# A state-space scan on one core: GpSimd multiplies the states by the C row in pairs of channel blocks

## The reference

```python
def step(state, xs):                       # 4 sequences of 512 positions
    d_t, B_t, C_t, u_t = xs                # 512 channels, 16 states each
    dA = exp(d_t[..., None] * A)
    state = state * dA + (d_t * u_t)[..., None] * B_t[:, None, :]
    y_t = einsum('ben,bn->be', state, C_t)
    return state, y_t
y = (y + D * u) * silu(layernorm(x))
x = x + tanh(g_xattn) * y
x = x + tanh(g_ffn) * moe(layernorm(x))    # top 6 of 16 experts, and two shared ones
```

## Time and profile before

| | us |
|---|---|
| median of 3 runs | 1610.62 (1610.51 to 1610.87) |
| the profiled execution's own time | 1612.12 |
| its span in the profile | 1610.3 |
| TensorE busy | 1371.0 (85%) |
| weight load busy | 1216.4 (76%) |
| GpSimd busy | 966.0 (60%) |
| VectorE busy | 812.2 (50%) |
| ScalarE busy | 781.2 (49%) |

### The profile page before, as it was taken

How to read it: one execution, slowest core, us unless ns; L and a number is a source line. 1 busy time by engine, 2 the same in 40 slices (tenths; PEclk the granted TensorE clock), 3 DMA queues, 4 the chain that set the end, 5 groups by cost and what they waited for, 6 DMA issues and landing times.

```text
span 1610.3 us, 31484 instructions
## 1 busy us (share of the span) xinstructions
PE 1371.0 (85%) x8088; PEld 1216.4 (76%) x8089; DVE 812.2 (50%) x1451; ACT 781.2 (49%) x1303; POOL 966.0 (60%) x658
## 2 busy tenths in 40 slices
PE   4477687677867776999979999999999999999993
PEld 1266576565656665988979999999999989999893
DVE  3586895887798585255223333333333333333331
ACT  2699687968768872433223333333333333323331
POOL 0276575656667685787855556666665655666631
PEclk9598798888978788999989999999999999999997
DMA  2212121112213123345363555555544555555445
GB/s 78 58 33 67 33 66 53 55 44 62 54 54 115 34 75 115 47 109 129 68 133 68 135 135 135 135 135 131 130 121 85 132 144 128 130 134 135 80 66 131
DMA packets 61040, 151.77 MB, mean 94 GB/s; under 512 B 13808, under 2 KB 14448, under 8 KB 58592
## 3 DMA queue, kind: packets, MB, share of 16 engines
q0 software_dynamic: 31024, 64.19, 21.4%
q1 hardware_dynamic: 29952, 86.78, 16.7%
HBM read 106.02 MB, written 49.25 MB: 96 GB/s over the span
## 4 chain that ended last, share of the span: by engine, by line
PE 50%; DVE 5%; POOL 5%; issue 4%; ACT 3%; DVEq 1%; ACTq 1%; DMA 0%; POOLq 0%
PE bank L1446 15%; PE bank L1426 14%; PE bank L1427 13%; PE bank L1414 3%; POOL token_lists L824 2%; PE bank L1435 2%; DVE hs L962 1%; POOL sums L811 1%; PE bank L1337 1%; ACT gt L643 1%; PE bank L1325 1%; DVEq L1159 1%; POOL w L790 1%; ACT dA L648 1%; POOL hc L758 1%
## 5 line engine op out<-in xcount | busy, mean ns | idle before, releaser
L758 POOL TENSOR_TENSOR hc<-hs,crow 128x512 f32<-128x512 f32 x256 | 322.1, 1284 | 190.3 <-DVE hs L962 148.8
L1426 PE MATMUL bank<-w,xh 128*128 (+1 forms) x1088 | 370.0, 341 | 8.6 <-DVE xl L1146 5.7
L962 DVE TENSOR_TENSOR_SCAN hs<-dA,bank 128x512 f32<-128x512 f32 x256 | 298.2, 1207 | 109.8 <-ACT dA L648 62.6
L1427 PE MATMUL bank<-w,xh 128*128 (+1 forms) x1088 | 353.1, 325 | 0.0
L811 POOL DMA_INDIRECT sums<-ys,aid x104 | 174.7, 1680 | 267.8 <-ACT ys L696 253.9
L1337 PE MATMUL bank<-ident,gt 128*128 128x128 f32 x1024 | 193.0, 320 | 131.9 <-DVE hs L962 67.5
L1446 PE MATMUL bank<-w,ah 128*128 (+1 forms) x816 | 268.9, 411 | 15.4 <-DVE al L1179 15.3
L1337 PEld LDWEIGHTS bank<-ident,gt 128*128 128x128 f32 x1024 | 140.5, 165 | 169.2 <-DVE hs L962 87.4
L1179 DVE TENSOR_TENSOR al<-bank,ah 128x384 fp32r<-128x384 f32 x136 | 75.9, 558 | 336.8 <-ACT ah L690 324.1
L1426 PEld LDWEIGHTS bank<-w,xh 128*128 128x128 f32 x1088 | 206.1, 189 | 33.2 <-issue 30.1
L1427 PEld LDWEIGHTS bank<-w,xh 128*128 128x128 f32 x1088 | 207.9, 191 | 2.4
(11 more groups left out here) (174 smaller groups left out, 1959.7 us busy)
## 6 DMA issues: line engine op xcount, KB each, us to landing
wraw<-in_wall SPq DMA_DIRECT2D x18, 2176.0 KB, 9.1
crow<-c_rows SPq DMA_DIRECT2D x64, 256.0 KB, 3.3
xt<-token_rows SPq DMA_DIRECT2D x32, 266.0 KB, 2.8
token_rows<-rowb SPq DMA_DIRECT2D x4, 1064.0 KB, 5.6
xrow<-in_x SPq DMA_DIRECT2D x4, 1024.0 KB, 7.0
sums<-xrow SPq DMA_DIRECT2D x4, 1024.0 KB, 4.3
ctxt<-in_ctxT SPq DMA_DIRECT2D x4, 512.0 KB, 5.1
xt<-token_rows,gid POOLq DMA_INDIRECT x104, 4.3
```

Source lines behind the costliest of these rows:

```text
L758: nc.gpsimd.tensor_tensor(hc[:, j, :], hs[:, j, :], crow[:, n % 4, :], ALU.mult).then_inc(hc_done, 1)
L962: nc.vector.tensor_tensor_scan(hs[:, j, :], dA[:, 4 * (n % 2) + j, :], dbu[j % 2][:], 0.0, ALU.mult, ALU.add).then_inc(scanned, 1)
L1426: nc.tensor.matmul(gate_bank[:, 0:I], xx, columns(w, off + ww + k * 2 * I, I), start=first, stop=last)
L1427: mm = nc.tensor.matmul(up_bank[:, 0:I], xx, columns(w, off + ww + k * 2 * I + I, I), start=first, stop=last)
```

## The change

GpSimd's step now takes the four channel blocks in two pairs. A pair is one instruction with 128x1024 elements: `hs[j]` and `hs[j + 1]`, which lie one behind the other, times the same row of C, read twice by a dimension of stride 0. It waits for the second scan of its pair and until TensorE has read both `hc` blocks of the step before. When it ends it raises `hc_done` by two. Nothing else is changed; the waits of the other engines for `hc_done` and `scanned` are written as they were.

```diff
@@ -751,11 +751,12 @@
         def _(pool):
             def step(b, n):
                 pool.wait_ge(crow_in[n % 4], 16 * (b * (DS // 4) + n // 4 + 1))
-                for j in range(J):
+                for j in range(0, J, 2):
                     i = (b * DS + n) * J + j
-                    pool.wait_ge(scanned, i + 1)
-                    at_least(pool, summed, i - 3)
-                    nc.gpsimd.tensor_tensor(hc[:, j, :], hs[:, j, :], crow[:, n % 4, :], ALU.mult).then_inc(hc_done, 1)
+                    pool.wait_ge(scanned, i + 2)
+                    at_least(pool, summed, i - 2)
+                    both = crow[:, n % 4, :].unsqueeze(1).to_broadcast([P, 2, L])
+                    nc.gpsimd.tensor_tensor(hc[:, j:j + 2, :], hs[:, j:j + 2, :], both, ALU.mult).then_inc(hc_done, 2)
```

## The result

The changed kernel takes 1635.4 us (median of 4 runs, 1627.9 to 1636.7), the kernel before 1610.6 beside it: ratio 1.0141, 95% interval 1.0116 to 1.0166. It is slower, as forecast, but by 22.7 us (from the ratio) to 24.9 (from the medians) where the forecast said 13.7, and 4 us above the end of the range.

The account below looks back on a forecast made before the run. GpSimd follows; ScalarE leads in middle steps, VectorE in steps 12 to 15 of batches 0 to 2. Terms 6.6 + 3.0 + 1.2 + 1.0 + 1.2 - 0.5 + 1.2 = 13.7 us give 1624.3 us, range 1615 to 1631.

Parts of the forecast that it names:

- steps 12 to 14: Batches 0 to 2: VectorE's delta instructions held longer behind the second pair; 6.6 us for steps 13 and 14, 3.0 for 12.
- step 11: Routing arithmetic on VectorE ends later behind the second pair: +1.0 us in batch 1, +0.2 in batch 2.
- the early steps at nothing: Steps 0 and 1: the pair ends 1.1 us later, but the convolution on VectorE hides it; no cost.
- L910's term: Step 4, last batch: four-column VectorE instruction that stood 2.82 us behind three products finds a gap; -0.5 us, bound +1.75.
- the end of the last batch: After step 12: GpSimd's products without a gap, +0.3 us, then more transposes behind the last pair, +0.9; sum 1.2.
- Steps 10 and 11: Last batch: VectorE's L1019 and routing copies stand longer behind the second pair; +1.0 and +1.2 us.
- what I cost at nothing: Hand-over of pairs to the next step's scans, steps 0 and 1, loads of C rows, other engines' queues: no cost.
- rival C: Much slower: the hand-over closes on itself in most steps; 1634 us, chance 9%.
- 4 us more from first scan to first scan of a batch: Sign that would show the forecast: each batch's distance between first scans grows by 4 us.

Follow-up runs that it names:

- pairs_in_8_to_11: Kernel before, with pairs only in steps 8 to 11 of batches 0 to 2, single products elsewhere: ratio 1.0008.
- pairs_in_0_to_7: Kernel before, with pairs only in steps 0 to 7 of batches 0 to 2: ratio 0.9996.
- pairs_in_batches_0_to_2: Changed kernel, with single products in the last batch and pairs in all steps of batches 0 to 2: ratio 1.0103.
- single_in_12_to_14: Changed kernel, with four single products in steps 12 to 14 of batches 0 to 2: ratio 1.0061 to the kernel before.
- late_singles: Changed kernel, with four single products that keep the waits and the signal of the pairs: 1629.6 us, ratio 1.0117 to the kernel before.
- first_pair_only: Changed kernel, with blocks 0 and 1 as a pair, blocks 2 and 3 singly, in every step: ratio 1.0062 to the kernel before.

## Why the prediction was right or wrong

**Right: the direction and its reason.** GpSimd follows, so its saved 19.8 us bought nothing; the price is VectorE standing still behind a product that ends later. Single product, pair and L949 came out at 1284, 2375 and 2740 ns where 2377 and 2750 were forecast.

**Right: steps 12 to 14.** 9.6 us forecast, 10.2 in the step table, 10.8 by the ratio of the kernel that has pairs there alone. **Right: step 11** (1.2; 1.3 us within 2.1 by pairs_in_8_to_11, though 2.1 in the step table of the changed kernel) **and the early steps at nothing** (-0.6 us, within 2.1, by pairs_in_0_to_7), although there TensorE and the scans wait more: the later steps of a batch take it back, as the -1.1 of step 6 shows.

**Off in size: L910's term.** With pairs, L911 found its gap and took 0.38 us instead of 2.82; for steps 2 to 4 together -1.6 us where the forecast took -0.5:

```profile
539.73 0.38 DVE L911 SCALAR_TENSOR_TENSOR nmr<-bag,rstd 128x4 f32<-128x4 f32 x1
```

**Wrong in a premise, nearly right in sum: the end of the last batch.** "From the last product of step 12 to its last product GpSimd has no gap": this was true of before and not of after. GpSimd, steps 13 and 14, and the first scans of step 15 on VectorE:

```profile
615.42 4.70 POOL L759 TENSOR_TENSOR hc<-hs,crow 128x1024 f32<-128x1024 f32 x2 [0.65 <-PE bank L1326]
620.08 1.35 POOL L772 TENSOR_TENSOR w<-wraw,w 128x544 fp32r<-128x544 f32 x1
621.38 4.67 POOL L759 TENSOR_TENSOR hc<-hs,crow 128x1024 f32<-128x1024 f32 x2
```
```profile
623.87 4.65 DVE L963 TENSOR_TENSOR_SCAN hs<-dA,bank 128x512 f32<-128x512 f32 x4 [1.28 <-POOL hc L759]
```

The pairs waited 0.65 us for TensorE. From the last product of step 12 to the end of the last product GpSimd now takes 20.85 us (611.11 to 631.96) where it took 20.0: +0.9 for a forecast of +0.3. TensorE's last transposes end 1.58 us behind that product where it was 0.86: +0.7 for +0.9. (The starts of the scans moved more, +2.4 us over steps 12 to 15, since they wait 1.28 us for a whole pair; but the end hangs on the products, and from the last scan's start to the last product's end it is now 4.6 us instead of 6.1.) Steps 10 and 11 grew by 1.4 and 1.1 (forecast 1.0 and 1.2). From the first scan of the batch to the last transposes the profiled execution lost 4.25 - 0.71 = 3.5 us where 2.9 were forecast. The ratio of pairs in the last batch alone, 1.0006, is less than that; the step from 1.0103 (without) to 1.0125 and 1.0141 (with) is more, with overlapping intervals. So the size stays open between 1 and 6 us.

**Wrong: "what I cost at nothing".** This is the step that failed. In the profiled execution steps 8 to 10 grew by 6.4 us, 5.7 of them in batches 1 and 2, where the sum had nothing; all the rest of its 23.3 us more together is only 3.2 above the sum of 13.7. The pairs in these steps cost little (1.0008 with step 11). The prediction had only compared the moment at which a pair's result is ready with the moment at which it is needed, taking each step by itself; it noted that in a few steps the cover is 0.3 us or less, and set no term for them. It left out that a batch that runs late can meet TensorE's lower level elsewhere: the earlier trace rows had it in the stage's mean of 0.85, but no term of the sum moved with it. Batches 1 and 2, the same in the changed kernel and in pairs_in_batches_0_to_2, differ by 3.7 and 3.6 us between the two executions, of which 3.3 and 3.2 lie in steps 8 to 10 and go with the clock (0.79 against 0.94). It was in rival C only as a tighter hand-over at a given clock, with a chance of 9%, and not as a term. C's time (1634) was near, its mechanism half: the lower level was in it, and the scans' waits for TensorE's transposes did grow, from 25.9 to 56.4 us. But C left the level where it had been and let the hand-over itself bind in 10 of 64 steps, so that its time comes out near is partly luck. The sign "4 us more from first scan to first scan of a batch" failed in the same way: it was 2.5, 7.4 and 8.3 us.

**What stays open.** The parts measured one by one are 0.0067 (steps 12 to 14), 0.0008 (8 to 11), -0.0004 (0 to 7) and 0.0006 (last batch), 0.0077 in all or 12.4 us: close to the forecast's 13.7. All together cost 0.0125 and 0.0141. With intervals of 0.0013 to 0.0033 on each, that surplus of 8 to 10 us is just outside what chance would make. It shows more clearly in single_in_12_to_14: pairs everywhere but in the nine steps cost 0.0061, while steps 8 to 11, 0 to 7 and the last batch, one by one, add up to 0.0010. Step 15 of batches 0 to 2 is in none of these parts and was not tried alone; its length changes by -1.0, +0.5 and 0.0 us in the changed kernel, which speaks against it as the source. The trace shows one way for the surplus to arise, the clock's place; and the changed kernel's executions, which spread over 12 us, have the lower mean clock where they are slower (0.929 at 1627.5 us, 0.922 at 1639.5). That this place is worse on average with pairs everywhere has not been shown; nor what decides where the level falls. So about half of the loss, the 10.8 us of steps 12 to 14, has a cause that is shown, and the surplus stays open.

## What to carry to other kernels

An engine that isn't the bound can still set the time by when its work ends: before merging two of its instructions, look at what the merged one must wait for and at which instructions of the other engine will now stand behind it. The same reading points to the gain: making GpSimd wait until VectorE's two-input instructions were through made the kernel 0.5 to 1.0% faster. And when a forecast is a sum of local holds, its range needs a term for all that moves with a late batch: in the profiled execution steps 8 to 10 moved by 6.4 us, and the sum's terms outside steps 12 to 14 came to 4.1.

## What the runs showed of the hardware

- VectorE's instruction with two inputs in SBUF (128x512, 0.69 us alone) ended 0.54 to 0.55 us behind GpSimd's instruction, whether that was one of 1.28 or of 2.41 us: it stands for the whole of it. The Trainium skill, Advanced Engine Details and Errata, section VectorE Performance Modes, says that the second Vector SBUF port is shared with GpSimd, and that GpSimd's instructions and VectorE's "2p" instructions "interfere/block" each other. The traces agree, here for a tensor_tensor with both inputs in SBUF (1.65 and 2.74 us instead of 0.69), and add how long it is held.
- In late_singles VectorE got exactly one instruction through between two GpSimd instructions in a row, and the second GpSimd instruction then took 1.72 instead of 1.27 us. It isn't always so: L910 of the kernel before stood 2.82 us through the ends of two products and got through only when the third ended. In steps 13 and 14 a single long instruction and two short ones cost VectorE nearly the same, 1.10 and 0.96 us a step.
- A tensor_scalar from SBUF to SBUF (L947, 0.40 us) can be held as well: 1.18 us in first_pair_only.
- The same stretch of work, steps 8 to 10 of a batch, took 28.7 to 29.2 us at a mean granted clock of 0.94 and 32.3 to 32.6 at 0.79, in a stage in which TensorE is busy 402 of 542 us.
- A row of C read twice by a stride of 0 costs GpSimd nothing: 2375 ns for 1024 columns, where the line through 544 and 4352 columns gives 2377.
